# Three stages in one block: loads of a stage issued in the one before, and a bias added during attention

## What is computed

```python
h = jnp.take(tok_weight, x, axis=0)                       # (4, 2048, 256)
n = layernorm(h)
ct_q, ct_kv = n @ Wd_q_w + Wd_q_b, n @ Wd_kv_w + Wd_kv_b  # 128 wide
query = heads(ct_q @ Wu_q_w + Wu_q_b) + heads(rope(ct_q @ Wq_r_w + Wq_r_b))
key   = heads(ct_kv @ Wu_k_w + Wu_k_b) + heads(rope(n @ Wk_r_w + Wk_r_b))
value = heads(ct_kv @ Wu_v_w + Wu_v_b)
h = h + merge(softmax(query @ key.T / scale) @ value) @ Wo_w + Wo_b
xt = layernorm(h)
probs = softmax(xt @ w_router); top1 = argmax(probs); gate = probs[top1]
slot = top1 * C + pos                                     # pos: how many took this expert before
y = (silu(buf @ w_gate) * (buf @ w_up)) @ w_down          # buf: the rows by slot
out = h + (xt + y[slot] * gate)                           # y only where pos < C
```

## Time and profile before

| | |
|---|---|
| median of 3 runs | 3409.88 us (3405.86 to 3410.36) |
| profiled execution: its own time, its span | 3416.31 us, 3414.5 us |
| PE busy | 3233.6 us (95%) |
| DVE busy | 2910.9 us (85%) |
| ACT busy | 2467.7 us (72%) |
| POOL busy | 565.0 us (17%) |
| DMA | 292.83 MB, 86 GB/s over the span |
| stage A | 0 to about 292 us |
| stage B | 295 to about 2970 us |
| stage C | 2971 to about 3153 us |
| stage D | from 3153 us |

### The profile page before, as it was taken

One profiled execution on the slowest core, in us unless ns is written; L12 is line 12 of the kernel. 1 busy time (PEld: TensorE's weight loads), 2 busy tenths in 40 slices (PEclk: granted clock), 3 DMA queues, 4 the chain that ended last, 5 costly groups with the idle time before them and its releaser, 6 DMA issues. The chain is left out here.

```text
span 3414.5 us, 67584 instructions
## 1 busy us (share of the span) xinstructions
PE 3233.6 (95%) x27520; PEld 1384.5 (41%) x27520; DVE 2910.9 (85%) x3156; ACT 2467.7 (72%) x4578; POOL 565.0 (17%) x753
## 2 busy tenths in 40 slices
PE   7995999999999999999999999999999999686998
PEld 3442333333333333333333333333333333375665
DVE  5776899999999999999999999999999999087232
ACT  3341588888888888888888888888888888532221
POOL 7882000000000000000000000000000000077233
PEclk9996799999999999999999999999999999897999
DMA  6886121212212020203121112111120200277562
GB/s 196 264 267 154 25 57 40 59 38 56 55 39 64 30 64 33 67 30 74 34 66 38 56 38 58 42 56 40 54 64 31 64 30 18 71 258 261 217 226 97
DMA packets 237736, 292.83 MB, mean 86 GB/s; under 512 B 44642, under 2 KB 165003, under 8 KB 232025
## 3 DMA queue, kind: packets, MB, share of 16 engines
q1 hardware_dynamic: 225392, 259.05, 27.1%
q0 software_dynamic: 12032, 29.45, 2.5%
HBM read 159.52 MB, written 132.94 MB: 86 GB/s over the span
## 5 line engine op out<-in xcount | busy, mean ns | idle before, releaser
L877 DVE TENSOR_REDUCE max_parts<-ps_m 128x2 f32<-128x1024 f32 x2048 | 2487.9, 1224 | 106.1 <-PE ps_m L731 95.1
L862 ACT ACTIVATE probs<-ps_s 128x512 f32<-128x512 f32 x4096 | 2216.3, 597 | 320.5 <-PE ps_s L762 190.0
L731 PE MATMUL ps_m<-keys,queries 48*128 48x512 f32 x4096 | 1493.8, 455 | 43.7 <-DMA queries<-halves_q 29.4
L762 PE MATMUL ps_s<-queries,keys 51*128 51x512 f32 x4096 | 1488.7, 449 | 12.7 <-DMA queries<-neg_rows 3.4
L779 PE MATMUL ps_o<-probs,vals 128*32 128x256 f32 x16384 | 1298.9, 392 | 0.0
L762 PEld LDWEIGHTS ps_s<-queries,keys 51*128 51x128 f32 x4096 | 611.7, 186 | 840.3 <-issue 793.2
L731 PEld LDWEIGHTS ps_m<-keys,queries 48*128 48x128 f32 x4096 | 598.2, 188 | 103.4 <-issue 55.8
L779 PEld LDWEIGHTS ps_o<-probs,vals 128*32 128x32 f32 x16384 | 329.7, 108 | 725.0 <-issue 706.3
L695 POOL TENSOR_TENSOR heads_out<-weighted,recip_rows 128x512 f32<-128x512 f32 x64 | 82.1, 1282 | 2213.7 <-DMA recip_rows<-recip_rows_dram 2213.7
L1550 DVE TENSOR_TENSOR hidden<-ps_u,silu 128x320 f32<-128x320 f32 x64 | 31.5, 492 | 135.6 <-PE ps_u L1482 135.6
L1526 ACT ACTIVATE silu<-ps_g 128x320 f32<-128x320 f32 x64 | 28.0, 437 | 148.7 <-PE ps_g L1482 148.7
(11 more groups left out here) (107 smaller groups left out, 1623.0 us busy)
## 6 DMA issues: line engine op xcount, KB each, us to landing
slot_rows<-empty SPq DMA_DIRECT2D x16, 1290.0 KB, 5.2
rows_d<-slot_rows SPq DMA_DIRECT2D x16, 1290.0 KB, 8.1
vext<-val SPq DMA_DIRECT2D x64, 256.0 KB, 4.6
halves_q<-parts SPq DMA_DIRECT2D x64, 256.0 KB, 3.5
halves_k<-parts SPq DMA_DIRECT2D x64, 256.0 KB, 3.1
keys<-halves_k SPq DMA_DIRECT2D x32, 512.0 KB, 7.8
queries<-halves_q SPq DMA_DIRECT2D x128, 128.0 KB, 3.2
vals<-vext SPq DMA_DIRECT2D x32, 512.0 KB, 5.5
```

The costliest lines, as they stand in the source:

```text
L731: mm = pe.matmul(ps_m[m % 2][:, h, :], queries_r[rows, par, qt, p, t * P:(t + 1) * P], keys_r[rows, par, p, c * 512:(c + 1) * 512], start= ...
L762: pe.matmul(ps_s[bank][:], keys_r[rows, par, p, k * P:(k + 1) * P], queries_r[rows, par, qt, p, :], start=True, stop=True).then_inc(scores ...
L862: act.activation(probs[:, n % RING, :], ps_s[bank][:], ACT.Exp, scale=SCALE).then_inc(probs_ok[bank], 1)
L877: dve.tensor_reduce(max_parts[:, lu % 2, :, p, t, c], ps_m[m % 2][:], AX.X, ALU.max).then_inc(maxima_ok[m % 2], 1)
```

## The change

1. Stages A, B and C become one block, with semaphores that are cleared once at its end. What kept the stages apart is replaced by waits on single semaphores of the stage in front (`FirstStage`, `Attention`): PE waits for the last copies out of the PSUM tiles that it takes over. Stage D keeps its own block.
2. The first quad's keys and queries are loaded in stage A, by SP behind the stores of chunks (1,2) to (2,3) (`first_loads`), into tiles of their own (`FirstHeads`, at the other end of SBUF); so `keys` and `queries` are two tiles each instead of one tile with two halves. POOL fills the tiles of ones and zeros in stage A. The first values are loaded at the start of stage B, behind the wait for all stores, as before.
3. The router's constants, the rows and heads of its first four chunks and their token numbers are loaded in attention (`RouterBuffers`).
4. The output bias is added in attention: in unit 0 of each quad SP loads 512 embedding rows, in unit 1 POOL adds the bias in place (`add_bias`), in unit 3 SP stores them back, last batch first. The first batch's stay in SBUF. The router stage has no `add_bias`; `residual` reads `emb`.
5. The last unit's division (`normalise_last`) is done by POOL in the router stage, between its first two `root`s.

```diff
@@ class RouterBuffers @@
+    def add_bias(self, pool, i):
+        k = i % CPB
+        pool.wait_ge(self.const_in, 16 * self.NCONST)
+        pool.wait_ge(self.emb_in[k], 16 * (i // CPB + 1))
+        pool.tensor_tensor(self.emb[:, k], self.emb[:, k], self.b_o[:].rearrange("p (a n) -> p a n", a=1).to_broadcast([P, CT, DM]),
+                           ALU.add).then_inc(self.bias_ok, 1)
@@ phase_a, SP (called behind chunk(b, k)) @@
+            def first_loads(b, k):
+                heads = first_heads
+                if (b, k) == (1, 2):
+                    for par in range(2):
+                        sp.wait_ge(parts_out[par], CPB // 2 * STORES * 16)
+                    heads.load_keys(sp, dram, heads.keys, 0, heads.early_in)
+                if (b, k) == (1, 3):
+                    heads.load_queries(sp, dram, heads.queries, 0, 0, heads.early_in)
+                if b == 2 and k > 0:
+                    heads.load_queries(sp, dram, heads.queries, 0, k, heads.stacks_in[0])
+                if (b, k) == (3, 0):
+                    sp.wait_ge(heads.ones_ok, 5)
+                    heads.load_ones(sp, heads.keys)
@@ phase_a, POOL @@
             pool.memset(val[:], 1.0).then_inc(ones_set, 1)
+            first_heads.fill(pool)
             pool.wait_ge(ids_in[2], 16)
@@ phase_b, SP @@
-            load_keys(0, 0, early_in)
-            load_queries(0, 0, 0, early_in)
-            for qt in range(1, SEQ // CH):
-                load_queries(0, 0, qt, stacks_in[0])
             load_vals(0, 0)
...
+            first_heads.load_ones(sp, keys[1])
             max_rows(0, 0)
+            sp.wait_ge(first_heads.ones_ok, 5)
+            router.load_const(sp, dram)
@@ phase_b, SP, step_of @@
+                    chunk = step * 2 + q
+                    b, k = BATCH - 1 - chunk // CPB, chunk % CPB
+                    if lu % 4 == 0:
+                        if chunk >= CPB:
+                            sp.wait_ge(router.emb_back[k], 16 * (chunk // CPB))
+                        router.load_emb(sp, dram, b, k)
                     if lu % 4 == 2:
                         clear_slots(step * 2 + q)
+                    if lu % 4 == 3 and b > 0:
+                        sp.wait_ge(router.bias_ok, chunk + 1)
+                        router.store_emb(sp, dram, b, k)
+                    if last and lu == 2:
+                        for i in range(2):
+                            sp.wait_ge(heads_out_done[i], CPB * UNITS // 4 * 16)
+                        for k in range(CPB):
+                            router.load_heads(sp, dram, 0, k)
+                        for k in range(3):
+                            router.load_tokens(sp, dram, 0, k)
@@ phase_b, POOL, step_of, behind the split of unit lu + 1 @@
+                    if lu % 4 == 1:
+                        router.add_bias(pool, step * 2 + lu // 4)
@@ phase_b, PE @@
-            pe.wait_ge(ident_ok, 1)
+            pe.wait_ge(stage.trans_copied, NCH)
+            pe.wait_ge(stage.latents_copied, 2 * NCH)
+            pe.wait_ge(stage.values_copied, 2 * NCH)
             for n in range(-LEAD, 0):
...
+            pe.wait_ge(ident_ok, 1)
+            pe.wait_ge(stage.terms_ok[1], 4 * NCH)
+            pe.wait_ge(stage.full_ok[1], 2 * NCH)
@@ phase_c, POOL @@
-            add_bias(0, 0)
-            add_bias(0, 1)
+            pool.wait_ge(proj_ps, 1)
             root(0, 0)
+            attention.normalise_last(pool)
             root(0, 1)
-            add_bias(0, 2)
...
-                if not (last and k + 3 >= CPB):
-                    add_bias(*nxt(b, k, 3))
@@ phase_c, PE @@
+            for i in range(2):
+                pe.wait_ge(attention.maxima_ok[i], QUADS * (SEQ // CH) * (SEQ // P))
             project(0, 0)
```

More of the change, by code:

```diff
@@ L65, in phase_a, with __init__ @@
+class Attention:
+    def __init__(self, sem):
+        self.maxima_ok = [sem(f"maxima_ok{i}") for i in range(2)]
+        self.probs_ok = [sem(f"probs_ok{i}") for i in range(3)]
+        self.heads_out_done = [sem("heads_out_done0"), sem("heads_out_done1")]
+        self.slots_out = sem("slots_out")
+        self.normalise_last = None
+def phase_a(nc, block, sem, dram, stage, first_heads):
     with ExitStack() as ctx:
@@ L450, in _, with phase_b @@
                 for k in range(CPB):
-                    chunk(BATCH - 1, k, True)
-def phase_b(nc, dram, out):
+                    chunk(b, k, False)
+            for k in range(CPB):
+                chunk(BATCH - 1, k, True)
+def phase_b(nc, block, sem, dram, stage, first_heads, router, attention):
     UNITS = 2 * (SEQ // CH)
@@ L496, in phase_b, with inner @@
     PER_BANK = PLACES[0][4]
[L498 removed]
+    with ExitStack() as ctx, ExitStack() as within:
         def sb(name, shape, dt=F32):
[L500 to L516 removed]
+            return router.ctx.enter_context(nc.sbuf_tensor(name, shape, dt))
+        def inner(name, shape, dt=F32):
+            return within.enter_context(nc.sbuf_tensor(name, shape, dt))
         weighted = sb("weighted", [P, 2, CH])
@@ L935, in load, with phase_c @@
                 sp.dma_start(dst[:, k, 2 * h:2 * h + 2], src[:, 2 * h:2 * h + 2]).then_inc(done[k], 16)
-def phase_c(nc, dram, out, experts):
-    NCONST = 6
+def phase_c(nc, block, sem, dram, out, stage, router, attention, experts):
+    NCONST = router.NCONST
     FAR = float(1 << 20)
@@ L1029, in phase_c @@
         place_ok = sem("place_ok")
-        near_ok = sem("near_ok")
         over_ok = sem("over_ok")
```

1735 lines of the change are left out of this document (881 added, 854 removed).

## The result

The changed kernel takes 3355.89 us at the median of 4 runs (3353.22 to 3360.46), beside 3410.12 us for the kernel before in the same session. The ratio is 0.9837, with a 95% interval from 0.9826 to 0.9849: 54 us faster. The forecast was 3349.9, with a range from 3335 to 3365. A second session gave 3358.09 and 0.9825 (0.9812 to 0.9839).

The account below looks back on a forecast made before the run. Attention was taken as filled by PE and DVE, with idle edges around it and a router stage paced by DVE. Terms -25 + 2 + 0 - 27.5 - 7.5 - 2 = -60 us took 3409.9 to 3349.9 us, range 3335 to 3365.

Parts of the forecast that it names:

- First seam, -25: Between stage one and attention: PE and DVE's idle gap of 25.6 us goes, 25 us off.
- Stage one, +2: Stage one takes on early key and query loads and POOL's memsets: together 2 us more.
- if stage one is over 5 us longer: A sign stated beforehand that the prediction is wrong: stage one lengthened by more than 5 us.
- I charge 1 us: Stage one: cost of 3.1 MB of moved loads, set against a free DMA share of 41 us; bounds 0 and 10.
- Rival 3: Moved loads crowd stage one, or bias additions touch attention: 10 us more, 3360; chance 0.20 shared with another rival.
- Attention, 0: Attention: 16 added bias additions, with row loads and stores, cost nothing; 38 us if each addition stopped DVE.
- Clock at the start: Start of attention's scores: PE's half-clock start-up, costing 8.1 us, stays whole after the change.
- Rival 1: PE's clock does not fall, or rises once scores fill PE: the 8.1 us go too, 3342; chance 0.13.
- Second seam, -27.5: Between attention and router: first residual 24.5 us earlier, first top logit 26, next interval 8.5 us; 27.5 us off.
- Router chunks, -7.5: Router stage: without bias additions, 11 chunks go from 9.18 to 8.5 us, PE becoming the bound; 7.5 us off.
- full-clock chunk without slack: Router stage: a chunk bound by PE at full clock, taken as 7.84 us.
- Last batch, -2: Router stage's last batch, which also loads experts at a DMA share of 0.98: 2 us off.

Follow-up runs that it names:

- lead_filled: Changed kernel with first key loads spread out, plus extra 48-row PE matmuls into an unused bank in the lead before attention's scores: 3349.85 us, ratio 0.9825.
- hole_filled: Changed kernel with keys spread, memsets later, router projection split, plus three full-row matmuls in PE's wait before the first scores: 3341.75 us, ratio 0.9790.
- bias_in_router: Changed kernel with its 16 bias additions back on POOL in the router stage, row loads and stores staying in attention: 3366.43 us, ratio 0.9862.
- split_project: Changed kernel with first key loads spread out, plus the first half of each router-stage projection moved ahead of the logits: 3337.89 us, ratio 0.9795.

## Why the prediction was right, and where its terms were off

**First seam, -25: right.** It measured 25.6. I named the barrier and the loads together; the runs divide them. Without early loads the removed barrier is worth 0.5 us, without the removed barrier the early loads 15.

**Stage one, +2: too small; 7.7 in one profile, 5.5 in the other (290.9).** By the prediction's own sign ("if stage one is over 5 us longer") it is wrong here. The failing step is "I charge 1 us" for the loads. The bounds, 0 and 10, held it. The free share of 41 us was the wrong measure: 1.5 MB in one row delay the store behind them, and POOL, DVE and PE wait for that store in turn; 6.0 us in the first profile, 4.3 in the second. The memsets, "about 1 us", are near that: 1.2 us on the mean of a start that scatters by more, and 1.0 at their other place. Rival 3's first half came true in part.

**Attention, 0: right.** Neither the units nor the tile `marked` show the additions; the share is 0.23 instead of 0.20.

**Clock at the start, "keep it whole": wrong as a rule.** The 8.1 us were one sample of a quantity that scatters between executions of one program. Rival 1's second half (it rises as soon as scores keep PE full) described this execution, but not the second one of the same program. The rule that I set beside it, of the Trainium skill, "TensorE: Matmul & The Clock Gate", Part 1, is that sustained activity releases the throttled clock. The runs agree with it only in part: behind 43 us of uninterrupted 48-row matmuls the clock was still 0.50 (lead_filled), behind 3 us of full-row ones it was 1.00 (hole_filled).

**Second seam, -27.5: near.** 24.8 to the first residual, as forecast; 2.3 to the first top instead of 1.6; but the next interval took 11.0 us, not 8.5, since a projection ran at half clock there. 26.1 in all.

**Router chunks, -7.5: right in size, and in cause for the slow half.** The other 14 intervals went from 9.16 to 8.52 us, where I had 8.5; bias_in_router gives the additions' price a second time. PE with its falling clock was named as the bound, and split_project confirms that the slow chunks were the excess over 7.87. But the "full-clock chunk without slack" of 7.84 us had slack: PE waits for ACT in it twice, 0.77 and 0.19 us, and in split_project 7.87 us stay although PE then waits 1.10. For the fast chunks PE's work alone is not the bound. Nor is `marked` the only operation there with two inputs from SBUF (`onehot` and `own_place` are others); it is the one that stands beside the addition. **Last batch, -2: wrong sign.** From the last `top` to the experts took 24.0 us, 1.9 more; in the twelve other executions it took 22.8 to 25.2. It is not that the chunks come faster, since bias_in_router, with chunks as slow as before, has 24.4; its cause stays open.

**The sum.** The profiles differ by 63.3, of which 11.3 (5.8 and 5.5) are steps that scatter. The other 52.0 stand to my 60 as: stage one +5.7, second seam +1.4, router chunks and last batch together +2.4, first seam -0.6, experts -1.1. The medians differ by 54.2 and, in the second session, 58.7. The two seams give 51.7 us; stage one's loss of 7.7 and the router stage's gain of 7.1 nearly cancel, where the forecast had a gain of 7.5 from the two. So the number came out near because the seams were sized well.

## What to carry to other kernels

A barrier and the loads behind it overlap: the barrier taken away alone moved 0.5 us here, the loads alone 15, both 25.6. So price each with the other still there, and move the loads first. Spread moved transfers out, one per period, and ask which store stands behind them on the queue and who waits for it; the free share of the transfers says only that they fit. Before a few us are put down to a change, look how far the same step lies apart in two executions of one program.

## What was not expected of the hardware

A busy TensorE can stay at half clock. In lead_filled the granted clock was 0.50 through 43 us of back-to-back matmuls with 48 rows; in hole_filled it rose within 3 us of matmuls with 128 rows and fell again 3.4 us later, in the scores with 51 rows. In the changed kernel's router stage it fell six times between 2955 and 3060, although PE never paused there for more than 0.77 us. In fourteen profiles it rose for good 1.9 to 29.8 us behind the first matmuls with 128 rows of the values. What decides between 2 and 30 us stays open. And one moved half-projection removed the falls in a whole stage without less work; why was not found.
